# Moving the scatter of an edge list between the stages of a graph network kernel

## The reference

```python
x = _layernorm(x + L0(x, edges))            # 5 attention convolutions, 4 heads of 32
x = _layernorm(x + L1(x, edges, types))     # relational attention, 4 edge types
x = _layernorm(x + L2(x, edges))            # two graph convolutions with normed degrees
x = _layernorm(x + L3(x, src, dst, weight)) # message to src: weight * (x @ W)[dst]
```

## Time and profile before

| | us |
|---|---|
| median of 3 runs | 6053.51 (6052.91 to 6057.18) |
| the profiled execution | 6050.8 |
| its span, first to last instruction | 6048.9 |
| POOL busy in it | 4069.1, 4166 instructions |
| of these: scatters of the list, L627 | 429.0, 416 instructions |
| PE busy | 3664.6 |
| DVE busy | 3438.1 |
| ACT busy | 1502.4 |

### The profile page before, as it was taken

One profiled execution on the slowest core, in us unless ns is written; L12 is line 12 of the kernel. 1 busy time (PEld: TensorE's weight loads), 2 busy tenths in 40 slices (PEclk: granted clock), 3 DMA queues, 4 the chain that ended last, 5 costly groups with the idle time before them and its releaser, 6 DMA issues. The chain is left out here.

```text
span 6048.9 us, 84275 instructions
## 1 busy us (share of the span) xinstructions
PE 3664.6 (61%) x17732; PEld 2882.4 (48%) x17733; DVE 3438.1 (57%) x9268; ACT 1502.4 (25%) x3527; POOL 4069.1 (67%) x4166
## 2 busy tenths in 40 slices
PE   5666667775666566668887366666344344455555
PEld 3555456654565355535664256654333233333443
DVE  7777656664666466656664476663343434345665
ACT  4343233432333233324553222221000000000000
POOL 4577577757775777757774776663677767746774
PEclk6788777776777777868887655555555555557777
DMA  7566266626563556546562433320211122212111
GB/s 232 169 186 176 82 198 179 186 84 189 173 187 113 166 173 178 158 124 177 170 177 54 109 71 67 69 60 2 57 53 53 34 57 53 53 31 62 52 52 44
DMA packets 629698, 681.61 MB, mean 113 GB/s; under 512 B 179329, under 2 KB 511762, under 8 KB 629010
## 3 DMA queue, kind: packets, MB, share of 16 engines
q0 software_dynamic: 166400, 384.50, 22.9%
q1 hardware_dynamic: 462994, 293.86, 16.8%
HBM read 620.45 MB, written 57.47 MB: 112 GB/s over the span
## 5 line engine op out<-in xcount | busy, mean ns | idle before, releaser
L613 POOL DMA_INDIRECT kvconv<-kv_tab,src_all x1664 | 1625.2, 977 | 644.7 <-issue 496.6
L613 POOL DMA_INDIRECT rowsg_<-h_tab,src_all x832 | 786.8, 946 | 300.7 <-issue 252.9
L627 POOL DMA_INDIRECT lst_tab<-pay,ord_now x416 | 429.0, 1031 | 452.1 <-issue 245.1
L613 POOL DMA_INDIRECT rowsw_<-h_tab,dst_i_w x416 | 399.8, 961 | 209.5 <-issue 120.1
L613 POOL DMA_INDIRECT rows_r<-rel_tab,idx_r x416 | 417.7, 1004 | 182.2 <-issue 114.9
L613 POOL DMA_INDIRECT kvlast<-kv_tab,src_all x416 | 409.9, 985 | 132.2 <-issue 122.8
L1051 ACT ACTIVATE Sconv<-s8conv 128x512 f32<-128x512 fp8e4 x384 | 240.8, 627 | 388.8 <-PE pA1conv L1009 275.8
L1113 DVE TENSOR_TENSOR msgconv<-kvconv,sm_attEconv 128x512 f32<-128x512 f32 x416 | 286.1, 688 | 77.1 <-PE pA0conv L1009 28.7
L1009 PEld LDWEIGHTS pA0conv<-Sconv,msgconv 128*128 128x128 f32 x1664 | 296.7, 252 | 12.9
L1009 PE MATMUL pA0conv<-Sconv,msgconv 128*128 128x128 f32 x1664 | 296.0, 338 | 0.0
L1009 PEld LDWEIGHTS pA1conv<-Sconv,msgconv 128*128 128x128 f32 x1664 | 282.9, 240 | 16.0
(11 more groups left out here) (705 smaller groups left out, 9033.5 us busy)
## 6 DMA issues: line engine op xcount, KB each, us to landing
qwinconv<-q_tab SPq DMA_DIRECT2D x1664, 64.0 KB
kvconv<-kv_tab,src_all POOLq DMA_INDIRECT x1664
st8conv<-st_tab SPq DMA_DIRECT2D x52, 512.0 KB
s8conv<-s_tab SPq DMA_DIRECT2D x52, 512.0 KB
qwinlast<-q_tab SPq DMA_DIRECT2D x416, 64.0 KB
kv_tab<-stageconv_n SPq DMA_DIRECT2D x28, 512.0 KB, 3.1
rowsg_<-h_tab,src_all POOLq DMA_INDIRECT x832
rel_tab<-stage_r SPq DMA_DIRECT2D x28, 272.0 KB, 4.2
```

The lines of the kernel that those rows point to most:

```text
L613: nc.gpsimd.indirect_dma_start(rows[:, par * TG + t, :], None, tab, bass.IndirectOffsetOnAxis(ap=idx[:, g * TG + t:g * TG + t + 1], axis=0 ...
L627: nc.gpsimd.indirect_dma_start(lst_tab, bass.IndirectOffsetOnAxis(ap=ord_now[:, i:i + 1], axis=0), pay[:, i, :], None).then_inc(sem("liste ...
```

## The change

The 416 scatters are divided anew. The arithmetic is the same, and so is the number of gathers.

| place | before | after |
|---|---|---|
| node block of each of the first four convolutions | 42 | 34 |
| edge block of the last convolution, after its gathers | 0 | 30 |
| node block of the last convolution | 38 | 32 |
| `rel_project` | 58 | 48 |
| after the gathers of each of 13 groups of `rel_edges` | 5 | 10 |
| after all gathers and scatters of `rel_edges` | 0 | 40 |
| node block of L1 | 50 | 0 |
| node block after the first graph convolution | 37 | 0 |

ord_now and pay hold 70 tiles instead of 58. In `rel_edges` the places and rows no longer fit at once: SP loads those of 60 tiles, and POOL, after group 5, waits until all scatters so far have landed and loads the next 70 itself; it waits for them after the gathers of group 6. At the end it does the same for the last 40.

```diff
-JOINT = 42
-LISTED = [CONVS * JOINT - 4, 58, 5 * GROUPS, 50, 37]
-MOST = max(LISTED[1:])
+JOINT = 34
+DRAIN = 30
+EACH = 10
+LISTED = [(CONVS - 1) * JOINT, DRAIN + 32, 48, EACH * GROUPS, 40]
+MOST = 70
...
-        def order_in(sp, first, count):
-            sp.dma_start(ord_now[:, 0:count], ord_tab[:, ds(first, count)]).then_inc(sem("ord_in"), 16)
-            sp.dma_start(pay[:, 0:count, :], edges_c[:, ds(first, count), :]).then_inc(sem("ord_in"), 16)
+        def order_in(eng, first, count, there="ord_in"):
+            eng.dma_start(ord_now[:, 0:count], ord_tab[:, ds(first, count)]).then_inc(sem(there), 16)
+            eng.dma_start(pay[:, 0:count, :], edges_c[:, ds(first, count), :]).then_inc(sem(there), 16)
...  in conv_edges
                     gather_all(pool, lambda g, par: gather_group(pool, tag, l, g, par, kv_tab, src_all, kv), since)
+                    if deg is not None:
+                        pool.wait_ge(sem("ord_in"), 32 * CONVS)
+                        list_rows(pool, DRAIN)
...  in node_stage
-                if kind in ("last", "rel"):
+                if kind == "last":
                     @block.gpsimd
                     def _(pool):
-                        nth, upto = (CONVS, 1) if kind == "last" else (CONVS + 3, 4)
-                        pool.wait_ge(sem("ord_in"), 32 * nth)
-                        list_rows(pool, JOINT - 4 if kind == "last" else LISTED[3])
-                        pool.wait_ge(sem("listed"), 16 * sum(LISTED[:upto]))
+                        list_rows(pool, LISTED[1] - DRAIN, DRAIN)
+                        pool.wait_ge(sem("listed"), 16 * sum(LISTED[:2]))
                 @block.sync
                 def _(sp):
-                    if kind == "rel":
-                        order_in(sp, sum(LISTED[:3]), LISTED[3])
...  in conv_last
-                    order_in(sp, l * JOINT, JOINT - 4)
+                    order_in(sp, LISTED[0], LISTED[1])
...  in rel_project
                     pool.wait_ge(sem("ord_in"), 32 * (CONVS + 1))
-                    list_rows(pool, LISTED[1])
-                    pool.wait_ge(sem("listed"), 16 * sum(LISTED[:2]))
+                    list_rows(pool, LISTED[2])
+                    pool.wait_ge(sem("listed"), 16 * sum(LISTED[:3]))
...
-                    order_in(sp, LISTED[0], LISTED[1])
+                    order_in(sp, sum(LISTED[:2]), LISTED[2])
...  in rel_edges
                         if g == 0:
                             pool.wait_ge(sem("ord_in"), 32 * (CONVS + 2))
-                        list_rows(pool, 5, 5 * g)
+                        if g == 6:
+                            pool.wait_ge(sem("ord_pool"), 32)
+                        list_rows(pool, EACH, EACH * (g if g < 6 else g - 6))
+                        if g == 5:
+                            pool.wait_ge(sem("listed"), 16 * (sum(LISTED[:3]) + 6 * EACH))
+                            order_in(pool, sum(LISTED[:3]) + 6 * EACH, 7 * EACH, "ord_pool")
                     gather_all(pool, group)
-                    pool.wait_ge(sem("listed"), 16 * sum(LISTED[:3]))
+                    pool.wait_ge(sem("listed"), 16 * sum(LISTED[:4]))
+                    order_in(pool, sum(LISTED[:4]), LISTED[4], "ord_pool")
+                    pool.wait_ge(sem("ord_pool"), 64)
+                    list_rows(pool, LISTED[4])
+                    pool.wait_ge(sem("listed"), 16 * T)
...
-                    order_in(sp, sum(LISTED[:2]), LISTED[2])
+                    order_in(sp, sum(LISTED[:3]), 6 * EACH)
...  in gcn_layer, node block of g1_
-                                @block.sync
-                                def _(sp):
-                                    order_in(sp, sum(LISTED[:4]), LISTED[4])
-                                @block.gpsimd
-                                def _(pool):
-                                    pool.wait_ge(sem("ord_in"), 32 * (CONVS + 4))
-                                    list_rows(pool, LISTED[4])
-                                    pool.wait_ge(sem("listed"), 16 * T)
```

## The result

The changed kernel takes 5937.82 us (median of 4 runs, 5934.87 to 5940.81), beside 6053.21 us for the kernel before on the same chip: a ratio of 0.9818, 95% interval 0.9806 to 0.983. The forecast of 5949.0 was 11.2 us too high. Its profiled execution took 5938.3 us, its span 5936.4, so the spans differ by 112.5 us.

A forecast was written before the change was run, and what follows sets the result against it. POOL was taken to end the node steps and, with ten scatters per group, to bound the relational pass just beyond DVE. Gains less 21.0 us gave 104.5, from 6050.8 to 5946.3, plus 2.7 for the median: 5949, range 5937 to 5969.

The forecast's parts named there:

- Price of one scatter: One scatter with its interval costs POOL 1.29 us in the relational pass, 1.275 us in node steps.
- I take the 5.1 us between them as landing and block change: First convolution node step, POOL's last scatter to SP's next load: 5.1 us, about 4.7 of it landing.
- S: Relational pass after group 5: POOL's stall for landing (4.7 us) and two plain loads (2.6), 7.3 us, bounds 5.4 to 12.
- POOL becomes the bound by a little: Relational pass with ten scatters: POOL's group takes 55.0 us against DVE's 54.26, so POOL sets the pace from group 1.
- Everything behind moves by 21.0: Relational pass: the last group reaches DVE 21.0 us later, and ScalarE's end moves equally, from 4166.2 to 4187.2.
- It ties with 4187.2, so these 40 cost nothing: Relational pass's tail: POOL's 40 scatters land at 4186.8, level with ScalarE's end at 4187.2, at no cost.
- Sum: Whole kernel: gains of 40.8, 7.65, 12.75, 37.5 and 26.8 us less 21.0 lost in the relational pass, 104.5 us.
- 1 (POOL keeps up): Relational pass: POOL's ten-scatter group takes 54.3 us or less, loss only 13 us, kernel 5941; chance 0.12.
- 2: Relational pass: POOL's tail ends it through slow loads or stretched scatters, loss 31 to 40 us, kernel 5959 to 5968; chance 0.15.
- 3: Convolution node steps: stores or late landing set their end, at most half of 40.8 us comes, kernel 5969; chance 0.04.
- Rival 4: Relational pass: DVE stretches scatters to 2.00 + 0.30 us, 178 us lost, kernel about 6106, slower than before; chance 0.03.
- The rule against the change: Relational pass: DVE's hold on the port pair shared with GpSimd would lengthen scatters; forecast went by the measured 986 ns instead.

The follow-up runs named there:

- experiment 2: Changed kernel with all 130 places of the relational pass loaded by SP at its start, so no stall after group 5: 5931.9 us, ratio 0.9806.
- experiments 1: Changed kernel with the 40 scatters behind the relational pass put back into the first GCN node step: 5963.1 us, ratio 0.9854.
- experiment 9: Changed kernel with a small POOL MEMSET (mark) behind its last scatter wait in four places: ratio 1.0022 on a slow chip, 5932.7 us (0.9801) on another.
- experiments 4: Changed kernel with eight scatters per group for ten, all loaded once by SP, 26 in the first GCN node step: 5936.0 us, ratio 0.9817.
- 10: Changed kernel with all scatters spread, including 30 in each of the loop's three drains, none in GCN: ratio 1.0061 on a slow chip, 5934.3 us (0.9806) on another.
- experiment 7: Changed kernel with 26 scatters for 34 in each of the first four convolution node steps, 32 in the GCN node step: 5947.8 us, ratio 0.9833.

## Where the prediction was right and where not

- *Price of one scatter, node steps, last convolution, projection, relational and GCN node steps.* Each within 1 us. The price of 1.27 us held to within 2.3 us in five different counts in the GCN node step (30.6 expected and 31.9 measured for 40, 62.4 and 64.7 for 65, 12.8 and 12.2 for 26, 20.4 and 21.0 for 32, 17.9 and 18.6 for 30).
- *"I take the 5.1 us between them as landing and block change, and about 4.7 us of it as landing."* Turned round: landing 1.3 us, change of block 3.2. The forecast read this in the first step alone; before the change SP's first instruction came 5.1, 9.4, 8.8 and 5.1 us behind POOL's last scatter in the four. It made no difference in the node steps, where only what changes counts, but it went into S, and into the tail.
- *The stall S of 7.3 us.* Mis-sized: 2.9 us in the trace, 2.4 by experiment 2. Landing 1.44 for 4.7, two loads 1.15 for 2.6.
- *POOL becomes the bound by a little, 55.0 against 54.26 us.* Right: 54.7 us a group without the stall (experiment 2: 95.2 to 696.7 over eleven), 57.0 with twelve, 52.0 with eight. POOL's work with S was 711.3 us for 719.3, so the last `leak` moved by 12.7 for 21.0. Of the 8.0 us of difference 4.4 are the stall; the gathers were also shorter than before (412.4 us for 417.7).
- *"Everything behind moves by 21.0."* Not so: the drain behind it became 4.5 us shorter (71.3 for 75.8), as I read it because less work is queued behind DVE when POOL sets the pace. The traces fit that: from the last `leak` to ScalarE's end are 71.1 to 72.5 us in all seven such runs with ten or twelve a group, with a tail or without, and 75.8 to 77.0 in the five with eight or fewer. What the work is, no run shows. The loss up to ScalarE's end is 8.2 us.
- *"It ties with 4187.2, so these 40 cost nothing."* The instructions behind POOL were sized wrongly in both directions. POOL's last scatter ended 4.6 us ahead of ScalarE rather than with it, yet cost 5.7 us, since 10.6 us lie behind it and not 4.7. That it is POOL's end is shown by experiments 1 and 2, that it is not the landing by 9.
- *Sum.* 21.0 was forecast for the pass and 14.0 came, which is 7.0 of the 8 us by which the profiled executions differ from the forecast of 104.5; the medians differ by 3 us more. That the pass was not further off is luck: the shorter drain (-4.5) and the late end of the block (+5.7), both put at nothing, nearly cancel.
- *Rivals.* 1 (POOL keeps up) is false, though its price of 13 is near what came. 2 came in part, and cheaply. 3 is out, since the four layers gave 41.7 us and not half of 40.8, and 4, since the scatters in the pass had a mean of 1005 ns. Rival 4's own limit is reckoned wrongly: from its 189 us of room comes 1.92 us a scatter, and the 1.97 us it gives need 12 x 12.2 + 40 x 1.29 = 198 us, which is the room that its other numbers give.
- *The rule against the change.* In the pass it does not show: 986 ns before, 1005 after. Elsewhere single scatters are held beside DVE in every trace (see the last section), but those places were the same before and after.

## What to carry to other kernels

Work moved into an idle engine's stretch is free until that engine's time per turn passes that of the bound, and then costs its full time: up to ScalarE's end, eight scatters a group cost 1 us in all, ten 7 to 8 and twelve 35, so the place of the bend (52.0, 54.7, 57.0 us beside 54.3) is worth more than a price for one. In a drain the room is not the time until the other engines end, but that less what the end of a block takes behind this engine; it has to be measured in the same kind of block (here 3.2 us in one and 9.3 in another).

A version calculated from experiments 4 and 10, with 20 scatters for 30 in the loop's three drains and 50 for 20 behind the pass, would save the 28 to 32 us there and stand at 5903 to 5906 us by that estimate; it was not run, and no version that was run is clearly faster than the kernel after.

## What the runs showed of the hardware

- The end of a block is dear when POOL was last. Behind POOL's last scatter or mark it was 9.3 us at the end of the relational pass and of three edge blocks, 3.2 us in the first and fourth convolution node step and 4.2 in the projection; it was 0.25 us behind ScalarE where that was last. Why it is longer behind stages with hundreds of gathers, no run tells. A DMA in flight is not the reason: from the end of the mark behind the pass to SP (4111.83 to 4121.09, experiment 9) the trace has no packet of any queue, not of instructions either.
- A turn of the loop comes on top. Behind the second and third node step the next layer started 7.5 and 7.2 us after POOL's mark for 3.2 (experiment 9), and 5.0 and 4.8 us after the landing of the last store for 0.6 and 0.7 (experiment 7): some 4 us either way. In these stretches stand five packets of the instruction queues, 2.8 to 3.5 us ahead of the next layer, and in those of the first step none. That they are what the turn waits for is likely and not shown. The queues between the second mark and the next layer (1364.65 to 1372.13; packets, MB, share):

```profile
q14 instruction: 4, 0.03, 1.5%
q8 instruction: 1, 0.02, 0.9%
```

- A plain load issued by POOL holds it for 0.57 us, and the last of a row of scatters was waited for 1.2 to 2.8 us.
- In each of the four convolution node steps of all 14 traces one scatter is long: 3.42 to 4.65 us. It began 0.1 to 1.3 us behind the start of the second RECIPROCAL of the step and, whenever it began, ended 1.38 to 1.40 us behind that one's end, 56 times in 56. So it is held by what DVE does there, and this is no coincidence. The length of the RECIPROCAL alone is not it: beside the first one of the step no scatter was longer than 1.05 us. The second stands directly between two TENSOR_TENSORs of xT and accconv, the first by itself; which of these instructions holds the scatter, no run shows. The first two node steps of the kernel after:

```profile
711.25 3.33 DVE L835 RECIPROCAL inv1conv_n<-inv1conv_n 4x512 f32<-4x512 f32 x1
712.48 3.49 POOL L629 DMA_INDIRECT lst_tab<-pay,ord_now  x1 [0.31 <-issue]
...
1337.07 3.33 DVE L835 RECIPROCAL inv1conv_n<-inv1conv_n 4x512 f32<-4x512 f32 x1
1337.15 4.64 POOL L629 DMA_INDIRECT lst_tab<-pay,ord_now  x1 [0.30 <-issue]
```

- Beside the four TENSOR_SCALARs of DVE that make the masks in the projection it is the same: in all 14 traces the scatter that meets one takes 1.8 to 2.5 us and ends 0.05 to 0.13 us behind it. One of them in the kernel after:

```profile
3287.70 2.00 POOL L629 DMA_INDIRECT lst_tab<-pay,ord_now  x1 [0.30 <-issue]
3288.05 1.58 DVE L1512 TENSOR_SCALAR mask_r<-t_f_r 128x1248 bf16<-128x1248 f32 x1
```
